# One-core macaron block: who adds the tail's and the first chunk's expert outputs, where an offset is computed, and the order of two ScalarE copies

## The reference, cut to what matters

```python
def _layernorm(x, eps=1e-5): return (x - mean(x)) / sqrt(var(x) + eps)
x = hidden_states                                # (1, 2048, 512) fp32
x = x + 0.5 * ffn(_layernorm(x))
x = x + attn(_layernorm(x))
x = x + 0.5 * ffn(_layernorm(x))
# ffn: 8 experts, top 2 by x @ gate_w.T + gate_b + bias, softmax over the two;
#      h = silu(x @ w1[e].T + b1[e]) (352 wide); y = h @ w2[e].T + b2[e]; gated sum of the two y
# attn: q, k, v by projection and causal convolution (4 taps), 6 heads of 128;
#      angles theta, psi from q, k; state = rotate(state, phi) * alpha + beta * rotate(v, psi);
#      out = rotate(state, -theta); out * rms norm * silu(g) @ Wo
```

## Time and profile before

| | |
|---|---|
| median of 3 runs | 855.35 us (854.61 to 855.52) |
| profiled execution | 854.93 us |
| its span, first to last instruction | 853.2 us |
| TensorE busy | 783.4 us (92%) |
| VectorE busy | 601.5 us (70%) |
| ScalarE busy | 364.2 us (43%) |
| GpSimd busy | 230.7 us (27%) |
| mean granted TensorE clock | 0.964 of full speed |
| phase 0 slots / attention / phase 1 slots / tail | about 64 to 262 / 262 to 612 / 643 to 830 / 830 to 853 us |

### The profile page before, as it was taken

How to read it: one execution, slowest core, us unless ns; L and a number is a source line. 1 busy time by engine, 2 the same in 40 slices (tenths; PEclk the granted TensorE clock), 3 DMA queues, 4 the chain that set the end, 5 groups by cost and what they waited for, 6 DMA issues and landing times.

```text
span 853.2 us, 14154 instructions
## 1 busy us (share of the span) xinstructions
PE 783.4 (92%) x4250; PEld 425.9 (50%) x4251; DVE 601.5 (70%) x1013; ACT 364.2 (43%) x631; POOL 230.7 (27%) x225
## 2 busy tenths in 40 slices
PE   8689899999998998997999999999718999999998
PEld 4336455555653444443444444445405666666653
DVE  6885656566654669999989998995884555555544
ACT  5855333444333436554544654533432323333222
POOL 3212644445422011001221011021112444444420
PEclk9899999999999997998999999999957999999999
DMA  8973648975734601700631201265556463333885
GB/s 314 396 275 134 250 129 328 337 264 157 261 137 111 161 0 53 146 1 10 113 56 20 63 13 21 71 221 144 218 197 219 155 218 116 118 111 112 298 280 209
DMA packets 44955, 137.27 MB, mean 161 GB/s; under 512 B 5488, under 2 KB 5488, under 8 KB 41584
## 3 DMA queue, kind: packets, MB, share of 16 engines
q1 hardware_dynamic: 27536, 86.38, 28.2%
q0 software_dynamic: 17376, 50.34, 21.4%
HBM read 85.32 MB, written 51.38 MB: 160 GB/s over the span
## 4 chain that ended last, share of the span: by engine, by line
PE 77%; DVE 13%; DMA 3%; ACT 2%; issue 2%; POOL 1%; SPq 0%; DVEq 0%; ACTq 0%; POOLq 0%
PE bank L644 63%; PE bank L638 5%; PE bank L737 3%; DMA space<-xn_rows,slot_src 2%; PE bank L900 2%; PE bank L687 1%; DVE space L1635 1%; DVE space L1632 1%; PE bank L803 1%; DVE space L1398 1%; DVE bst L1389 1%; POOL space L565 1%; DMA space<-x_in 1%; DVE space L1458 1%; PE bank L883 0%
## 5 line engine op out<-in xcount | busy, mean ns | idle before, releaser
L644 PE MATMUL bank<-space 128*128 (+3 forms) x2958 | 579.4, 348 | 22.2 <-DVE space L1462 12.8
L644 PEld LDWEIGHTS bank<-space 128*128 128x128 f16 (+1 forms) x2958 | 273.1, 99 | 273.9 <-issue 26.7
L569 POOL DMA_INDIRECT y_rows<-space,slot_dst x78 | 86.2, 1105 | 159.8 <-DVE space L1530 159.2
L565 POOL DMA_INDIRECT space<-xn_rows,slot_src x78 | 81.9, 1050 | 127.1 <-PE bank L638 67.5
L1511 DVE TENSOR_TENSOR space<-bank,space 128x512 f16<-128x512 f32 x78 | 54.0, 692 | 80.3 <-issue 40.2
L1083 ACT ACTIVATE space<-space 128x352 f32<-128x352 f32 x78 | 38.8, 497 | 152.8 <-DVE space L1517 152.8
L1517 DVE SCALAR_TENSOR_TENSOR space<-bank,space 128x352 f32<-128x352 f32 x78 | 40.9, 525 | 63.7 <-PE bank L644 44.8
L638 PE MATMUL bank<-ident,space 128*128 128x128 f32 x440 | 67.6, 284 | 12.6 <-DMA space<-xn_rows,slot_src 10.7
L1530 DVE TENSOR_SCALAR space<-bank,slot_gate 128x512 f32<-128x512 f32 x78 | 58.5, 750 | 19.3 <-PE bank L644 13.4
L1088 ACT ACTIVATE space<-bank 128x384 f16<-128x384 f32 x78 | 38.3, 491 | 72.8 <-PE bank L737 72.3
L1632 DVE SCALAR_TENSOR_TENSOR space<-space,cang 128x512 f32<-128x512 f32 x84 | 63.1, 751 | 5.4 <-ACT space L1178 3.2
(11 more groups left out here) (197 smaller groups left out, 762.1 us busy)
## 6 DMA issues: line engine op xcount, KB each, us to landing
space<-ffn_w SPq DMA_DIRECT2D x8, 1472.0 KB, 9.8
w_saved<-space SPq DMA_DIRECT2D x8, 1472.0 KB
space<-w_saved SPq DMA_DIRECT2D x8, 1472.0 KB, 9.5
xn_rows<-space SPq DMA_DIRECT2D x8, 1024.0 KB, 6.2
space<-y_rows SPq DMA_DIRECT2D x16, 512.0 KB, 5.8
space<-x_in SPq DMA_DIRECT2D x7, 1024.0 KB, 11.8
space<-att_w SPq DMA_DIRECT2D x12, 518.0 KB
space<-y_rows POOLq DMA_DIRECT2D x6, 1024.0 KB, 9.1
```

The lines of the kernel that those rows point to most:

```text
L565: gp.indirect_dma_start(dst, None, rows, bass.IndirectOffsetOnAxis(ap=index, axis=0)).then_inc(done, 16)
L569: gp.indirect_dma_start(y_rows, bass.IndirectOffsetOnAxis(ap=slot_dst[:, t:t + 1], axis=0), yo[:, t % 2], None).then_inc(y_st[t % 2], 16)
L644: last = pe.matmul(dst, a, b, start=(n == 0), stop=(n == len(terms) - 1))
```

## The change

Four edits. *Tail*: VectorE adds 11 of the 16 tiles (`BY_DVE`), TensorE 5 (`BY_PE`); VectorE's first addition for its first five tiles is moved ahead of its last `y_out`; TensorE's first term of tile 2 is moved ahead of its last `down`; loads of the two outputs get semaphores of their own; the stores follow `OUT_ORDER`. *First chunk*: VectorE adds tiles 0 and 1 in SBUF, and the first output to tile 2; TensorE adds tile 3 and the rest of tile 2; ScalarE copies two tiles instead of four; three small memsets are moved behind the second `moments`. *Attention*: `offset` of the next chunk is moved into `convolve`, between the turn and the value taps. *Slots*: ScalarE's order `x_high(t+2)`, `silu(t+1)` holds in every tile of both phases.

```diff
-FIRST_BANKS = (3, 5, 7, 4)
-SUM_BANKS = (0, 1, 3, 5, 2, 4, 7, 6)
+FIRST_BANKS = {2: 5, 3: 3}
+BY_PE = (2, 5, 8, 11, 14)
+BY_DVE = tuple(n for n in range(NT) if n not in BY_PE)
+HEAD_START = 5
+OUT_ORDER = (0, 1, 2, 3, 4, 6, 5, 7, 9, 8, 10, 12, 11, 13, 15, 14)
+SUM_BANKS = (3, 0, 1, 5, 2)
...
                 if c == 0:
-                    sp.wait_ge(c_sum, TPC)
+                    sp.wait_ge(c_half, 3)
+                    sp.wait_ge(c_sum, 2)
...
# TensorE
                 ht(t + 2, 0)
-                if not ph:
-                    first_part(0, "x")
-                    first_part(0, 0)
-                    first_part(1, "x")
+                if ph:
+                    last_part(0, "x")
+                else:
+                    first_part(3, "x")
                 down(t + 2, 0, then)
...
             def first_rest():
-                first_part(0, 1)
-                first_part(1, 0)
-                first_part(1, 1)
-                for i in (2, 3):
-                    for k in ("x", 0, 1):
-                        first_part(i, k)
+                first_part(2, "x")
+                first_part(2, 1)
+                first_part(3, 0)
+                first_part(3, 1)
...
+            def last_part(m, k):
+                n = BY_PE[m]
+                g, i = divmod(n, TPC)
...
+                last = pe.matmul(bank[SUM_BANKS[m]][:, :], ident[:, :], rows, start=k == "x", stop=k == 1)
+                if k == 1:
+                    last.then_inc(f_pe, 1)
...
# ScalarE, slots: in every tile
                     h_high(t, par)
                     x_high(t + 2, par)
                     silu(t + 1, 1 - par)
...
# VectorE, end of slots
                 h_low(t + 2, 0)
+                if ph:
+                    for n in BY_DVE[:HEAD_START]:
+                        last_sum(n, 0)
+                else:
+                    for i in range(3):
+                        first_sum(i, 0)
                 y_out(t + 2, t // 2 + 1, 0)
+
+            def first_sum(i, k):
+                rows = group_rows[0][:, i]
+                v.wait_ge(yf_in[k], 16)
+                if k:
+                    v.tensor_tensor(rows, rows, y_first[:, 1, i], ALU.add).then_inc(c_half, 1)
+                    v.wait_ge(c_half, i + 2)
+                else:
+                    v.wait_ge(cg_in, 16)
+                    last = v.tensor_tensor(rows, rows, y_first[:, 0, i], ALU.add)
...
+            def last_sum(n, k):
...
+                v.wait_ge(yl_in[k][n // 2], 16)
+                last = v.tensor_tensor(rows, rows, y_last[:, k, n], ALU.add)
...
             def first_chunk():
-                first_stats(0)
-                first_stats(1)
+                ch.wait()
+                for i in (0, 1):
+                    first_sum(i, 1)
+                    first_stats(i)
                 ch.wait()
                 moments(0, 2)
...
                 moments(2, TPC)
+                v.wait_ge(w_save, 16 * E)
+                v.memset(raw[:, :, :, 0:HALO], 0.0)
+                v.memset(carry, 0.0)
+                ch(v.memset(sigab, 0.0))
                 first_low(0)
...
                 v.tensor_tensor(a, a, tmp[:, 1], ALU.subtract).then_inc(c_frac, 1)
+                if behind:
+                    behind()
                 v.wait_ge(c_ev, KINDS * u + 4)
                 value_tap(0, 0)
...
-                    if p == 0 and c < NCH - 1:
-                        offset(NCH + c + 2, 0, c_rstd)
+                    shift = (lambda: offset(NCH + c + 2, 0, c_rstd)) if p == 0 and c < NCH - 1 else None
+                    convolve(u + 1, (lambda: gate_low(u - 1)) if u else None, shift)
...
-            for n in range(0, NT, 2):
...
+            ch.wait()
+            for n in BY_DVE[:HEAD_START]:
+                last_sum(n, 1)
+            for n in BY_DVE[HEAD_START:]:
+                last_sum(n, 0)
+                ch.wait()
+                last_sum(n, 1)
```

More of the change, by code:

```diff
@@ L511, in _ @@
                     outputs_in(k, q)
-            for n in range(NT):
+            for n in OUT_ORDER:
                 sum_out(n)
@@ L1110, in slots @@
                 for t in range(2 * PEELED):
[L1111 to L1114, removed]
+                    step(t, t % 2)
                     if not ph and t < E - OWN - BYPE:
@@ L1137, in normalise @@
                     act.wait_ge(c_xt, TPC * c + i - 1)
-                rows = group_rows[c][:, i] if c else bank[FIRST_BANKS[i]][:, :]
+                rows = group_rows[c][:, i] if c or i < 2 else bank[FIRST_BANKS[i]][:, :]
                 act.activation(xnt[:, i % 2], rows, ACT.Identity, scale=rstd[:, 0, 0, i:i + 1],
@@ L1373, in _ @@
             slots(1)
-            for m in range(NT // 2):
+            for m in range(len(BY_PE)):
                 last_rows(m)
@@ L1573, in slots @@
                 h_low(t + 2, 0)
-                y_out(t + 2, t // 2 + 1, 0)
+                if ph:
+                    for n in BY_DVE[:HEAD_START]:
+                        last_sum(n, 0)
+                else:
+                    for i in range(3):
+                        first_sum(i, 0)
+                y_out(t + 2, t // 2 + 1, 0)
+            def first_sum(i, k):
[4 more added lines that the diff above has]
+                    v.wait_ge(c_half, i + 2)
+                else:
+                    v.wait_ge(cg_in, 16)
+                    last = v.tensor_tensor(rows, rows, y_first[:, 0, i], ALU.add)
+                    if i == 2:
+                        last.then_inc(c_half, 1)
+                    else:
+                        ch(last)
+            def last_sum(n, k):
+                g, i = divmod(n, TPC)
+                rows = rows_last[g][:, i]
+                if not k and g < NCH - 1:
+                    v.wait_ge(g_in[g], landed(g, 3))
+                v.wait_ge(yl_in[k][n // 2], 16)
+                last = v.tensor_tensor(rows, rows, y_last[:, k, n], ALU.add)
+                if k:
+                    last.then_inc(f_sum, 1)
+                else:
+                    ch(last)
             def variance(rows):
@@ L1596, in first_stats @@
             def first_stats(i):
-                v.wait_ge(c_first, i + 1)
-                ch(v.bn_stats(bst[:, i], bank[FIRST_BANKS[i]][:, :]))
+                if i < 2:
+                    rows = group_rows[0][:, i]
+                else:
+                    v.wait_ge(c_first, i - 1)
+                    rows = bank[FIRST_BANKS[i]][:, :]
+                ch(v.bn_stats(bst[:, i], rows))
             def first_low(i):
@@ L1624, in sigmoids_low, with convolve @@
                 v.tensor_tensor(sigab[32:32 + NAB], abs_[0:NAB], sigab[0:NAB], ALU.subtract).then_inc(c_sgl, 1)
-            def convolve(u, between=None):
+            def convolve(u, between=None, behind=None):
                 p, par = u % PAIRS, u % 2
@@ L1795, in _ @@
             slots(0)
[L1797 to L1800, removed]
             attention()
```

54 lines of the change are left out of this document (22 added, 32 removed).

## The result

The changed kernel takes 841.35 us (median of 4, 840.33 to 841.97) against 855.42 beside it: ratio 0.9836, interval 0.9819 to 0.9853. The profiled execution took 840.33 us with a span of 838.6.

The account below looks back on a forecast made before the run. TensorE was taken to bound the second expert pass, a chain changing engines attention, short serial stretches the tail and first chunk. 8.1 + 2.2 - 0.9 + 1.1 = 10.5 off 854.93, plus 0.42, gave 844.8 us; range 842.8 to 847.6.

Parts of the forecast that it names:

- Part 1: Tail: with sums shared anew, TensorE's and VectorE's work both ends at 842.0; gain 8.1 us, bounds 6.5 to 8.6.
- The stores did not become the bound: Tail rival: output stores queue and set the end, giving 846.6 us; chance 0.13.
- Part 2: First chunk's normalisation: earlier down product and statistics gain 2.8 us, less 0.6 for TensorE's clock: 2.2, bounds 1.0 to 3.0.
- the term for the clock: First chunk: TensorE's clock falling in the thin stretch adds about 0.5 us twice; 0.6 taken off.
- The VectorE order: First chunk: VectorE runs sum, statistics, sum, statistics; second statistics start at 261.8 against 262.84.
- The warning that the longer thin stretch brings the fall forward: Before the logits: TensorE's thin stretch grows to 262.4 to 271.6, so its clock may fall during it.
- Part 3: Attention, offset inside the convolution: first chunk costs 0.9 us, second gains 1.1, third 0; sum a gain of 0.2.
- rival 4: Attention, second chunk: with shorter idle TensorE keeps its clock, another 1.0 us off, 843.8; chance 0.10.
- Part 4: Expert slots, high rows ahead of SiLU: 0 us; gain excluded by TensorE's 164.84 of 165, loss needs 0.6 more.

## Why the prediction was wrong, by its own steps

- **Part 1, the tail: right.** Forecast 8.1, measured 8.17 in the trace and 7.7 by the medians with the old tail. VectorE's and ScalarE's last results came within 0.3 us of each other, as worked out, and the end 3.0 us behind, as allowed. The stores did not become the bound, but were close to it: the DMA engines were full, and the median landing was 0.4 us longer.
- **Part 2, the first chunk: right in its steps; the term for the clock was too small.** Forecast 2.2, measured 1.45 in the profiled execution, 1.4 to 2.1 over eight traces, 1.7 by the medians. The VectorE order came out as worked out. At full clock the stretch took 16.41 us (run with added products), 2.75 less than before, where 2.8 was forecast. The half clock then took 1.30 of it back in the profiled execution, 0.66 ahead of the last offset and 0.64 between it and the logits, and 0.6 in others; I had worked out about 0.5 twice and took only 0.6 off. The warning that the longer thin stretch brings the fall forward was right. The Trainium skill's rule that idle gaps between bursts bring the half clock back (TensorE: Matmul & The Clock Gate, Why this matters for your kernels) agrees with the granted 0.53 over 262 to 276, a stretch in which TensorE idled 2.80 and 2.29 us, and with the full clock that 25 idle products kept.
- **Part 3, the offset: right in mechanism and place, wrong in the sign of the sum.** The stall cost 1.06 (forecast 0.9), the second chunk gave 0.65 to 0.73 (forecast 1.1), the third nothing. I carried ScalarE's idle of 1.28, less 0.2, over to the chain. TensorE's idle did shrink by 1.40, but only half of that reached the fifth unit's squares; where the rest went no run shows. TensorE's clock stayed at half (0.52 over 396 to 403; before, 0.51 over 397 to 404), so rival 4 did not come about.
- **Part 4, the high rows ahead of SiLU: wrong, and this is what put the time outside the range.** The step that failed is "TensorE is full, so the earlier high rows give nothing". It took the busy share of a pipelined engine for proof that nothing holds it. It checked the consumer of the instruction that comes later (the transposes of SiLU's result: 0.6 us of slack, and indeed no wait) and not those of the one that comes earlier: low rows, then the up product. It even excluded a gain by the 164.84 of 165 us. The earlier trace rows shows the high rows held until 732.52 by SiLU; their own consumers, at 733.14 and 733.97, were not looked up. The term measured 4.5 to 4.8 us.

Against the forecast the parts are off by +0.1, -0.75, -0.6 and +4.8 us, and the time by 3.5. Size by size, 8.2 + 1.45 - 0.4 + 4.8 is 14.05 us, and the difference of the medians is 14.07. That this fits to the hundredth is luck: by the medians alone the parts are 7.7, 1.7, -0.6 and 4.8, or 13.6, and the changed kernel itself took 841.35 us once and 842.11 another time.

## What to carry to other kernels

A busy share of nearly 100% on TensorE is no proof that it waits for nothing: compare the step from tile to tile with the shortest one in the trace, and look for starts that follow another engine's end by a constant time, 0.14 us here. When an order is changed, follow both instructions to their consumers, the one that gets earlier as much as the one that gets later. In an engine's list, put what is ready ahead of what waits. Where TensorE must idle ahead of dense work, idle products can cost less than the half clock: 2.8 us were gained ahead of the first logits. Where another engine set the pace they only moved the idle, and with it the fall of the clock, to a worse place: 1.7 us were lost at the next change of chunk. And a trace is one execution: where the clock moves from one to the next, a stretch of 1 us is to be read from several.

## What the runs showed of the hardware that was not expected

GpSimd's instruction for the last scatter took 4.18 us (line L578 in the tail's rows), where the one at 820.34 took 0.97. Meanwhile VectorE ran sums with both inputs in SBUF, at first independent ones 0.60 us apart. The instruction took 4.17 or 4.18 in all eleven traces with this tail. In the three with the tail of before VectorE ran such sums beside it too, but every second one waits for the one ahead (steps of 0.72 and 0.61 us), and it took 1.17, as between the single sums of the first chunk. In this kernel nothing waits for it. The Trainium skill (SBUF — State Buffer, Who interferes with whom) says that such VectorE instructions contend with GpSimd ones that read SBUF, not with ones that only write it; the trace agrees in direction, for an instruction that writes DMA descriptors. No run here separates reading from writing, nor the spacing of the sums from their dependence.
